# Token mixer with a second x buffer, first sums ahead of the second products, rows normalised by ScalarE, and weight preparation behind two maps

## Chip, cores and metric

The kernel runs on one core of a Trainium2 chip. The time is that of the whole program on the device, in microseconds, so lower is better. Engines are named as in the profile: PE is TensorE (matrix products), PEld its weight loads, DVE is VectorE, ACT is ScalarE, POOL is GpSimd, SP issues the loads and stores. The engines run their own instruction lists in order and meet only at semaphores.

## What is computed

The program runs a token mixer, a linear attention, a quantised feed-forward, an agent attention and a mixture of experts, one after the other. The change touches the token mixer and the first step of the attention. The mixer in the reference, shortened (8 batches of 256 rows, 4 heads of 64):

```python
q = proj(Wq_w, Wq_b)
k = proj(Wk_w, Wk_b)
v = proj(Wv_w, Wv_b)
ew = jnp.exp(w_bias * local_mask)
ek = jnp.exp(k)
num = jnp.einsum('ts,nsd->ntd', ew, ek * v)
den = jnp.einsum('ts,nsd->ntd', ew, ek)
y = jax.nn.sigmoid(q) * num / den
h = y @ out_w + out_b + _flatten(x)
mu = jnp.mean(h, axis=-1, keepdims=True)
var = jnp.mean(jnp.square(h - mu), axis=-1, keepdims=True)
return (h - mu) * jax.lax.rsqrt(var + 1e-05) * ln_g + ln_b
```

The attention maps q and k by elu(u) + 1, keeps a decayed running sum of k for its denominators, and multiplies its result by a gate. The feed-forward has a weight that is rounded to three values with a scale per row; its preparation (absolute sums, limits, comparisons, diagonals) is done once.

## The kernel before

**Order.** Each engine's list is written by hand. In `token_mixer` all engines go through the 8 batches by `skewed` (L70): it calls a function `step(b, s1, s2, s3)` for b = -2, -1, 0, then in a hardware loop for 1 to 5, then for 6 and 7. In step b an engine does the first part of batch b+2 (s1), the second part of batch b+1 (s2) and the third part of batch b (s3). `skewed` also places single pieces between the steps.

**A batch.** SP loads x transposed into `a_xt`, a single buffer (`load_x`, L194). TensorE makes q, k and v of all heads (`qkv_products`, L234, product L243) into the PSUM banks 0 to 3. ScalarE takes exp(k) into `a_nk` (L316) and exp(-q) into `a_eq` (L320); VectorE multiplies exp(k) by v (`weigh`, L361). TensorE multiplies both by exp(w_bias) (`sums`, L266). VectorE forms the denominator (`den`, L368), its reciprocal (L370) and `y` (L372). TensorE turns y (`turn`, L254), ScalarE copies it to `a_yt` (`copy_yt`, L325), TensorE multiplies by out_w (`project`, L277). VectorE adds x and the bias, prepared by POOL in `a_xb`, into `a_hp` (L379), takes mean and variance (L383, L387) and `ve` (L389). POOL raises that to -1/2 (`root`, L433), VectorE normalises two tiles into `a_hn` (L395), POOL applies gain and bias (`gain`, L438 and L440) and splits an eighth of the attention's weights (`split`, L446), whose rounded half ScalarE has cast (L336).

**Step b of each list.** TensorE: products of b+2, turn of b, sums of b+1, project of b. ScalarE: copy of b, exponentials of b+2, cast. VectorE: `weigh(b+2)`, `den` and `y` of b+1, then `norm(b)` (L379 to L395). POOL: root of b, xb of b+1, gain of b, split. Between steps 5 and 6 VectorE takes the statistics of the attention's first rows (`rows_sums(0)`), between steps 6 and 7 those of the next (`rows_sums(1)`), and ScalarE normalises the first rows with their text tile (`rows_norm(0)`, L570). After its last step ScalarE does `rows_round(0)` (L598) and `rows_norm(1)`; VectorE does `rows_split(0)` (L605) inside `norm(7)`, before the wait for the last root, and ends with the last gain and bias (L409, L411).

**First attention step.** A barrier parts the mixer from `attention_and_ffn`. Its step b = -1 runs the projections of batch 0 on TensorE: pairs 0 and the values, pair 1, the text values (which wait for the first map), pairs 2 to 5, then the products of `ffn_weights`. ScalarE takes exp and relu of each pair (L1092, L1096). VectorE makes the map `phi` from both (L1253), and behind it a scan (L1259) or a product with the running sum (L1264). In VectorE's list `ffn_weights` (L1298) stands ahead of `phi(0, 0)`; it waits for the feed-forward's weights, which SP loads after the barrier.

## Time and profile before

| what | us |
|---|---|
| median of three runs | 705.87 |
| lowest and highest run | 705.17, 706.28 |
| profiled execution, its time | 705.16 |
| profiled execution, its span | 703.4 |
| PE busy | 576.3 (82%) |
| DVE busy | 443.1 (63%) |
| ACT busy | 258.9 (37%) |
| POOL busy | 211.1 (30%) |

The profile is of one execution. The busy shares are means over stages with different limits: the mixer is the first 115 of the 703 us, and what bounds it has to be read there. Times in the trace are counted from the start of the span. A row of the timeline gives start and duration, the engine and the line of the kernel, output and inputs, how many instructions were merged, and in brackets how long the engine stood idle before it and whose end released it. The clock of TensorE is given as a share of 2.4 GHz; it has two levels, so 0.84 means that part of the stretch ran at 1.2 GHz. For the first 30 us the profile has no clock record, and the rate is to be read from the products themselves.

### The profile page before, as it was taken

To read this page: it belongs to the slowest core of one execution; us is meant where nothing else is said; L and a number is where in the kernel's file an instruction comes from. 1 tells how busy PE (TensorE), PEld (TensorE's weight loads), DVE (VectorE), ACT (ScalarE), POOL (GpSimd) and SP (SyncE) were. 2 spreads that over 40 slices of the span, in tenths; PEclk is the share of its full clock that TensorE was granted. 3 is DMA by queue.
4 is the path that set the end of the run, shared out by engine and by line. 5 is a ranking of instruction groups with operands and counts; after the bars stand their busy time and mean duration, and the time that the engine had idled before them with its cause. 6 is when DMAs were issued, how large, how long until landed. Compare 5 with 4: busy or idle time off the path is not lost. (4 is left out here: it accounts for less than half of the span.)

```text
span 703.4 us, 10705 instructions
## 1 busy us (share of the span) xinstructions
PE 576.3 (82%) x3633; PEld 458.8 (65%) x3633; DVE 443.1 (63%) x1037; ACT 258.9 (37%) x541; POOL 211.1 (30%) x283
## 2 busy tenths in 40 slices
PE   4889957789998999899998955452899799999883
PEld 4566535647685868677767643221688699988782
DVE  1388886666877878778887753457768442322256
ACT  1511222326372727263645323310441045554410
POOL 2336554121111111001111000461201277777600
PEclk9999987789999999999999986556899899999997
DMA  6211112000000000000000060310300133333376
GB/s 203 81 45 45 44 46 69 22 1 1 1 1 1 2 1 1 1 1 1 1 1 1 1 225 0 79 34 10 104 23 1 31 95 104 103 107 106 90 225 194
DMA packets 27439, 36.97 MB, mean 53 GB/s; under 512 B 4541, under 2 KB 22782, under 8 KB 27390
## 3 DMA queue, kind: packets, MB, share of 16 engines
q1 hardware_dynamic: 23166, 24.78, 11.5%
q0 software_dynamic: 4224, 11.54, 5.4%
q8 instruction: 30, 0.49, 0.3%
q14 instruction: 19, 0.16, 0.1%
HBM read 25.95 MB, written 10.35 MB: 52 GB/s over the span
## 5 line engine op out<-in xcount | busy, mean ns | idle before, releaser
L611 PE MATMUL ps<-b_x_hi,wa_hi 128*128 128x288 f32 x192 | 59.6, 310 | 6.9 <-DVE w1raw L1253 3.0
L1450 POOL TENSOR_TENSOR c_rstd<-c_ve,mhalf 128x2 f32<-128x2 f32 (+1 forms) x16 | 11.9, 742 | 165.2 <-DVE c_ve L510 165.2
L2373 DVE TENSOR_TENSOR w1raw<-ps,w1raw 128x192 f32<-128x192 f32 x43 | 15.4, 358 | 68.6 <-ACT w1raw L2174 68.6
L612 PE MATMUL ps<-b_x_lo,wa_hi 128*128 128x288 f32 x192 | 58.1, 303 | 0.0
L613 PE MATMUL ps<-b_x_hi,wa_lo 128*128 128x288 f32 x192 | 57.9, 302 | 0.0
L2433 POOL DMA_INDIRECT kv<-x_rows,r_src_i x43 | 41.8, 972 | 28.4 <-DVE r_src_i L2295 11.1
L2060 PE MATMUL ps<-w,w1raw 96*128 x172 | 44.7, 382 | 1.2 <-ACT w1raw L2186 1.2
L1497 POOL TENSOR_TENSOR w1raw<-w1raw 128x288 f32<-128x288 f32 x16 | 15.4, 981 | 98.5 <-DVE w1raw L1253 98.5
L1126 ACT CAST b_y_hi<-b_yt 128x256 fp32r<-128x256 f32 x32 | 12.8, 399 | 86.5 <-DVE b_yt L1235 86.5
L611 PEld LDWEIGHTS ps<-b_x_hi,wa_hi 128*128 128x128 f32 x192 | 37.5, 195 | 10.0 <-DVE w1raw L1253 4.3
L1247 DVE TENSOR_TENSOR w1raw<-ps,decay 128x1024 f32<-128x1024 f32 x32 | 38.6, 1205 | 7.5 <-PE ps L934 7.5
L934 PE MATMUL ps<-w1raw 64*128 64x160 f32 (+2 forms) x384 | 41.5, 334 | 1.2 <-DVE w1raw L1284 1.2
L1253 DVE SCALAR_TENSOR_TENSOR w1raw<-b_ex,w1raw 128x576 f32<-128x576 f32 x32 | 25.3, 791 | 21.2 <-ACT w1raw L1096 21.2
L612 PEld LDWEIGHTS ps<-b_x_lo,wa_hi 128*128 128x128 f32 x192 | 37.5, 195 | 0.3
L934 PEld LDWEIGHTS ps<-w1raw 64*128 64x128 f32 (+1 forms) x384 | 27.1, 162 | 16.3 <-issue 9.5
L613 PEld LDWEIGHTS ps<-b_x_hi,wa_lo 128*128 128x128 f32 x192 | 37.6, 196 | 0.0
L266 PE MATMUL ps<-a_nk,a_ewt 128*128 (+1 forms) x64 | 37.0, 732 | 0.0
L243 PE MATMUL ps<-a_wqkv,a_xt 65*128 65x192 f32 x128 | 27.5, 378 | 8.9 <-DMA a_wqkv<-in_wqkv 5.7
L951 PE MATMUL ps<-w1raw,b_v 128*64 128x288 f32 (+1 forms) x256 | 32.8, 380 | 0.8 <-DVE w1raw L1247 0.8
L611 PE MATMUL ps<-w_hi,f_w 128*128 x86 | 32.7, 380 | 0.8 <-DVE f_w L2304 0.8
L243 PEld LDWEIGHTS ps<-a_wqkv,a_xt 65*128 65x128 f32 x128 | 25.9, 226 | 10.1 <-DMA a_xt<-in_x_t 9.4
L1092 ACT ACTIVATE b_ex<-ps 128x576 f32<-128x576 f32 x32 | 20.9, 652 | 30.4 <-PE ps L613 30.4
(380 smaller groups left out, 1604.7 us busy)
## 6 DMA issues: line engine op xcount, KB each, us to landing
d_x_hi<-y_rows SPq DMA_DIRECT2D x18, 256.0 KB, 3.9
w1raw<-in_W_t SPq DMA_DIRECT2D x8, 384.0 KB, 6.0
x_rows<-w1raw SPq DMA_DIRECT2D x6, 384.0 KB, 2.5
a_xt<-in_x_t SPq DMA_DIRECT2D x8, 256.0 KB, 3.3
a_xfl<-in_x_flat SPq DMA_DIRECT2D x8, 256.0 KB, 2.7
out<-hres SPq DMA_DIRECT2D x16, 128.0 KB, 3.6
w<-in_W_t SPq DMA_DIRECT2D x8, 192.0 KB, 3.8
w1raw<-in_Ws_t SPq DMA_DIRECT2D x1, 768.0 KB, 10.3
```

The source lines that it names most:

```text
L243: mm = nc.tensor.matmul(qkv[:, lt, h, 0:3 * F], xt[:, h, lt * P:(lt + 1) * P], wqkv[:, :], start=True, stop=True)
L266: mm = nc.tensor.matmul(ps[:, 4 + t, :], ewt[:, s, t * P:(t + 1) * P], nk[:, b % 2, s, :], start=s == 0, stop=s == 1)
L611: nc.tensor.matmul(out, x_hi, w_hi, start=start, stop=False)
L612: nc.tensor.matmul(out, x_hi, w_lo, start=False, stop=False)
L613: return nc.tensor.matmul(out, x_lo, w_hi, start=False, stop=stop)
L934: mm = nc.tensor.matmul(ps[keys, bank(j) + r, col:col + n], qk[rows, NP + j, s * P:s * P + m], qk[rows, j, T - n:T], start=True, stop=True)
L951: mm = nc.tensor.matmul(ps[DK * r:DK * r + DK, 6 + j % 2, T - n:T], v[:, s, h * DK:(h + 1) * DK] if s < 2 else v_text[keys, h * DK:(h + 1) ...
L1092: nc.scalar.activation(ex[:, i % 2], ps[:, group(i):group(i) + 2, 0:T], ACT.Exp)
L1247: nc.vector.tensor_tensor(a[:, j % 2], ps[:, bank(j):bank(j) + 2, 0:AW], g["decay"][:, 2 * j:2 * j + 2, :], ALU.mult).then_inc(masked, 1)
L1253: nc.vector.scalar_tensor_tensor(out=qk[:, qk_tiles(i), 0:T], in0=ex[:, i % 2], scalar=1.0, in1=qk[:, qk_tiles(i), 0:T], op0=ALU.min, op1= ...
L2060: mm = nc.tensor.matmul(ps[:, 6 + u, 0:D], e_ht[:, u, k, :], w2[:, k, bass.ds(e, 1), :].rearrange("p a f -> p (a f)"), start=k == 0, stop= ...
L2433: pool.indirect_dma_start(xg[j % NX], None, x_rows, bass.IndirectOffsetOnAxis(ap=src_i[:, j:j + 1], axis=0)).then_inc(gathered[j % NX], 16)
```

## The change

Four things. `a_xt0` is a buffer of its own for batch 0, so that the load of batch 1 is issued with the first loads, without a wait, and batches 2 and later wait as before for the products of the batch ahead. In step -1, TensorE does the sums of batch 0 before the products of batch 1, and VectorE the division of batch 0 before `weigh(1)`. The rows are normalised by two ScalarE activations, scale and shift per row, at the end of ScalarE's step; VectorE adds the negated mean, POOL the product of it with the root. In the first attention step `ffn_weights` stands behind `phi(0, 0)` and `phi(0, 1)` in VectorE's list. Besides, `setup` uses one semaphore less.

```diff
@@ -116,6 +116,7 @@
         lng = sb("a_lng", [P, D])
         lnb = sb("a_lnb", [P, D])
         xt = sb("a_xt", [F + 1, H0, L])
+        xt0 = sb("a_xt0", [F + 1, H0, L])
         xfl = sb("a_xfl", [P, 2, D])
         xb = sb("a_xb", [P, 2, D])
         nk = sb("a_nk", [P, 2, 2, 2 * D])
@@ -131,6 +132,8 @@
         ve = sb("a_ve", [P, 2, 1])
         tick = sb("a_tick", [P, 1])
         rstd = sb("a_rstd", [P, 2, 1])
+        nmu = sb("a_nmu", [P, 2, 1])
+        shift = sb("a_shift", [P, 2, 1])
         lgam = sb("a_lgam", [P, HA])
         age = sb("a_age", [P, T])
         agm = sb("a_agm", [P, T])
@@ -140,6 +143,7 @@
         ln_in = sem("a_ln_in")
         ew_in = sem("a_ew_in")
         x_in = sem("a_x_in")
+        x0_in = sem("a_x0_in")
         xf_in = sem("a_xf_in")
         attw_in = sem("a_attw_in")
         txt_in = g["rows"]["txt_in"]
@@ -196,7 +200,11 @@
                     xs = x_t[b]
                 else:
                     xs = x_t[bass.ds(b, 1)].rearrange("a c h l -> (a c) h l")
-                ge(sp, qkv_done, b)
+                if isinstance(b, int) and b == 0:
+                    sp.dma_start(xt0[0:F], xs).then_inc(x0_in, 16)
+                    return
+                if not isinstance(b, int) or b > 1:
+                    sp.wait_ge(qkv_done, b)
                 sp.dma_start(xt[0:F], xs).then_inc(x_in, 16)
 
             def load_flat(b):
@@ -208,13 +216,13 @@
             sp.dma_start(wqkv[:], ins["wqkv"]).then_inc(w_in, 16)
             sp.dma_start(ewt[:], ins["w_bias_t"].rearrange("(s p) t -> p s t", p=P)).then_inc(ew_in, 16)
             sp.dma_start(mask8[:], ins["mask_t"].rearrange("(s p) t -> p s t", p=P)).then_inc(ew_in, 16)
+            load_x(1)
             sp.dma_start(draw[:], row_broadcast(ins["decay_log"], HA)).then_inc(gam_in, 16)
             sp.dma_start(outb[:], row_broadcast(ins["out_b"], D)).then_inc(ln_in, 16)
             sp.dma_start(outw[:], ins["out_w"].rearrange("(c p) n -> p c n", p=P)).then_inc(ln_in, 16)
             sp.dma_start(lng[:], row_broadcast(ins["ln_g"], D)).then_inc(ln_in, 16)
             sp.dma_start(lnb[:], row_broadcast(ins["ln_b"], D)).then_inc(ln_in, 16)
             load_flat(0)
-            load_x(1)
             for i, n in enumerate(("W_Q_t", "W_K_t", "W_V_t", "W_g_t")):
                 sp.dma_start(stage[:, :, i * DA:(i + 1) * DA],
                              ins[n].rearrange("(c p) n -> p c n", p=P)).then_inc(attw_in, 16)
@@ -232,22 +240,26 @@
         @block.tensor
         def _(pe):
             def qkv_products(b):
-                ge(pe, x_in, 16 * b + 16)
+                x = xt0 if isinstance(b, int) and b == 0 else xt
                 if isinstance(b, int) and b == 0:
+                    pe.wait_ge(x0_in, 16)
                     pe.wait_ge(filled, 1)
+                else:
+                    pe.wait_ge(x_in, 16 * b)
+                if isinstance(b, int) and b == 0:
                     pe.wait_ge(w_in, 16)
                 ge(pe, ekv_done, b)
                 ge(pe, exps_done, b)
                 for lt in range(2):
                     for h in range(H0):
-                        mm = nc.tensor.matmul(qkv[:, lt, h, 0:3 * F], xt[:, h, lt * P:(lt + 1) * P],
+                        mm = nc.tensor.matmul(qkv[:, lt, h, 0:3 * F], x[:, h, lt * P:(lt + 1) * P],
                                               wqkv[:, :], start=True, stop=True)
                 mm.then_inc(qkv_done, 1)
 
             def turn(b):
                 pe.wait_ge(y_done, b + 1)
                 if isinstance(b, int) and b == 0:
-                    pe.wait_ge(g["ident_ready"], 1)
+                    pe.wait_ge(g["ident_ready"], 2)
                 ge(pe, yt_done, b)
                 for fc in range(FC):
                     for t in range(2):
@@ -279,6 +291,10 @@
                 mm.then_inc(out_done, 1)
 
             def step(b, s1, s2, s3):
+                if isinstance(b, int) and b == -1:
+                    sums(0)
+                    qkv_products(1)
+                    return
                 if s1:
                     qkv_products(b + 2)
                 if s3:
@@ -319,6 +335,14 @@
                 ge(act, y_done, b - 1)
                 nc.scalar.activation(heads(eq[:, b % 2]), part(0), ACT.Exp, scale=-1.0).then_inc(exps_done, 1)
 
+            def norm(b):
+                act.wait_ge(rstd_done, 2 * b + 2)
+                ge(act, gain_steps, 2 * b)
+                for t in range(2):
+                    last = nc.scalar.activation(hn[:, t, :], hp[:, t, :], ACT.Identity, bias=shift[:, t, :],
+                                                scale=rstd[:, t, :])
+                last.then_inc(hn_done, 1)
+
             def copy_yt(b):
                 act.wait_ge(turned, b + 1)
                 ge(act, out_done, b)
@@ -334,6 +358,7 @@
                     if isinstance(b, int) and b == 0:
                         act.wait_ge(attw_in, 16 * 4)
                     nc.scalar.copy(part_of(g["wa_hi"], b), part_of(stage, b)).then_inc(hi_done, 1)
+                    norm(b)
 
             skewed(act, step, (rates, decays, None, lambda: rows_norm(nc, g, act, 0)))
             rows_round(nc, g, act, 0)
@@ -341,6 +366,7 @@
 
         @block.vector
         def _(dve):
+            nc.vector.memset(xt0[F:F + 1], 1.0)
             nc.vector.memset(xt[F:F + 1], 1.0).then_inc(filled, 1)
 
             def rates():
@@ -376,6 +402,7 @@
                 dve.wait_ge(out_done, b + 1)
                 dve.wait_ge(xb_done, b + 1)
                 ge(dve, hn_done, b)
+                ge(dve, rstd_done, 2 * b)
                 nc.vector.tensor_tensor(hp[:].rearrange("p t f -> p (t f)"), ps[:, 7, :],
                                         xb[:].rearrange("p t f -> p (t f)"), ALU.add).then_inc(hp_done, 1)
                 dve.wait_ge(hp_done, b + 1)
@@ -386,17 +413,16 @@
                 for t in range(2):
                     last = nc.vector.bn_aggr(mv[:, t, :], stats[:, t, :])
                 step(last)
+                nc.vector.tensor_scalar(nmu[:], mv[:, :, 0:1], -1.0, None, ALU.mult)
                 nc.vector.tensor_scalar(ve[:], mv[:, :, 1:2], LN_EPS, None, ALU.add).then_inc(var_done, 1)
                 if isinstance(b, int) and b == B - 1:
                     rows_split(nc, g, dve, 0)
-                dve.wait_ge(rstd_done, b + 1)
-                ge(dve, gain_steps, 2 * b)
-                for t in range(2):
-                    last = nc.vector.tensor_scalar(hn[:, t, :], hp[:, t, :], mv[:, t, 0:1], rstd[:, t, :],
-                                                   ALU.subtract, ALU.mult)
-                last.then_inc(hn_done, 1)
 
             def step(b, s1, s2, s3):
+                if isinstance(b, int) and b == -1:
+                    divide(0)
+                    weigh(1)
+                    return
                 if s1:
                     weigh(b + 2)
                 if s2:
@@ -432,6 +458,8 @@
                 pool.wait_ge(var_done, b + 1)
                 nc.gpsimd.tensor_tensor(rstd[:], ve[:], g["mhalf"][:, 0:2].rearrange("p (t a) -> p t a", a=1),
                                         ALU.pow).then_inc(rstd_done, 1)
+                pool.wait_ge(rstd_done, 2 * b + 1)
+                nc.gpsimd.tensor_tensor(shift[:], nmu[:], rstd[:], ALU.mult).then_inc(rstd_done, 1)
 
             def gain(b):
                 pool.wait_ge(hn_done, b + 1)
@@ -482,14 +510,13 @@
 def setup(nc, g):
 
     with ExitStack() as ctx:
-        zeroed = ctx.enter_context(nc.semaphore("zeroed"))
         block = ctx.enter_context(nc.Block())
 
         @block.gpsimd
         def _(pool):
             nc.gpsimd.memset(g["mhalf"][:], -0.5)
-            nc.gpsimd.memset(g["ident"][:], 0.0).then_inc(zeroed, 1)
-            pool.wait_ge(zeroed, 1)
+            nc.gpsimd.memset(g["ident"][:], 0.0).then_inc(g["ident_ready"], 1)
+            pool.wait_ge(g["ident_ready"], 1)
             nc.gpsimd.affine_select(out=g["ident"][:], in_=g["ident"][:], compare_op=ALU.not_equal,
                                     fill=1.0, base=0, pattern=[[-1, P]],
                                     channel_multiplier=1).then_inc(g["ident_ready"], 1)
@@ -1415,14 +1442,14 @@
                     rows_split(nc, g, dve, b + 2)
                 if is_batch(u):
                     scale(u)
-                if b == -1:
-                    ffn_weights()
                 if is_batch(n):
                     phi(n, 0)
                 if is_batch(b):
                     split_y(b)
                 if is_batch(n):
                     phi(n, 1)
+                if b == -1:
+                    ffn_weights()
                 if is_batch(u):
                     quantise(u)
                 if is_batch(n):
```

## Rows read from the trace of the kernel before

**Rows 1.** windows: length, busy PE, PEld, DVE, ACT, POOL (count), PEclk, DMA share, GB/s

```profile
50.51:61.36 10.85, 10.11 (x37) 6.67 (x37) 8.76 (x14) 2.08 (x4) 5.72 (x5) 0.84 0.20 49
61.36:71.03 9.67, 8.42 (x37) 6.01 (x37) 8.67 (x14) 2.08 (x4) 5.71 (x5) 1.00 0.20 54
```

**Rows 2.** timeline, short loop step: start, us, engine, line, operation [idle <-releaser]

```profile
60.61 0.69 DVE L372 TENSOR_TENSOR a_y<-ps,a_rden 128x512 f32<-128x512 f32 x1
...
61.85 3.60 PE L266 MATMUL ps<-a_nk,a_ewt 128*128 x8
...
62.05 0.59 ACT L325 COPY a_yt<-ps 128x512 f32<-128x512 f32 x1 [8.65 <-PE ps L254]
...
63.01 0.17 DVE L389 TENSOR_SCALAR a_ve<-a_mv 128x2 f32<-128x2 f32 x1
...
63.02 0.60 ACT L320 ACTIVATE a_eq<-ps 128x512 f32 x1
...
63.26 0.70 POOL L433 TENSOR_TENSOR a_rstd<-a_ve,mhalf 128x2 f32<-128x2 f32 x1 [4.39 <-DVE a_ve L389]
...
63.99 1.67 DVE L395 TENSOR_SCALAR a_hn<-a_hp,a_mv,a_rstd 128x256 f32<-128x256 f32 x2 [0.81 <-POOL a_rstd L433]
...
65.29 1.89 PE L277 MATMUL ps<-a_outw,a_yt 128*128 128x256 f32 x8
...
65.59 0.67 DVE L361 TENSOR_TENSOR a_nk<-a_nk,ps 128x512 f32 x1
...
66.19 0.68 DVE L368 SCALAR_TENSOR_TENSOR a_den<-a_eq,ps 128x512 f32<-128x512 f32 x1
```

**Rows 3.** timeline, VectorE in the step at 0.84 clock

```profile
56.50 0.69 DVE L368 SCALAR_TENSOR_TENSOR a_den<-a_eq,ps 128x512 f32<-128x512 f32 x1 [1.08 <-PE ps L266]
```

**Rows 4.** timeline, shift and normalising of attention rows on POOL and ScalarE

```profile
109.97 0.20 POOL L560 TENSOR_TENSOR b_shift<-b_nmu,b_rstd 128x2 f32<-128x2 f32 x1
...
110.25 1.09 ACT L570 ACTIVATE b_xn<-hres,b_shift,b_rstd 128x256 f32<-128x256 f32 x2
```

**Rows 5.** timeline, TensorE in the mixer's first 31 us

```profile
14.38 5.49 PE L243 MATMUL ps<-a_wqkv,a_xt 65*128 65x192 f32 x16 [3.19 <-DMA a_xt<-in_x_t]
...
19.66 5.56 PE L266 MATMUL ps<-a_nk,a_ewt 128*128 128x512 f32 x8
...
25.06 2.77 PE L243 MATMUL ps<-a_wqkv,a_xt 65*128 65x192 f32 x16
...
30.11 0.86 PE L254 MATMUL ps<-ident,a_y 128*128 128x128 f32 x4 [2.29 <-DVE a_y L372]
```

**Rows 6.** timeline, VectorE and ScalarE at the mixer's end

```profile
97.38 0.69 DVE L368 SCALAR_TENSOR_TENSOR a_den<-a_eq,ps 128x512 f32<-128x512 f32 x1
...
103.38 0.59 ACT L325 COPY a_yt<-ps 128x512 f32<-128x512 f32 x1 [0.78 <-PE ps L254]
...
107.88 0.68 DVE L379 TENSOR_TENSOR a_hp<-ps,a_xb 128x512 f32<-128x512 f32 x1
...
114.23 0.69 DVE L411 TENSOR_TENSOR hres<-a_hn,a_lnb 128x512 f32<-128x512 f32 x1
```

**Rows 7.** timeline, all engines in the first step of attention

```profile
119.40 0.66 ACT L1096 ACTIVATE w1raw<-ps 128x576 f32<-128x576 f32 x1
...
123.12 0.17 DVE L1304 COPY fold<-ident 32x32 f32<-32x32 f32 x1 [4.76 <-issue]
...
124.29 0.64 ACT L1096 ACTIVATE w1raw<-ps 128x576 f32<-128x576 f32 x1
...
127.43 0.75 DVE L1253 SCALAR_TENSOR_TENSOR w1raw<-b_ex,w1raw 128x576 f32<-128x576 f32 x1
...
131.84 0.61 PE L611 MATMUL ps<-b_x_hi,wa_hi 128*128 128x288 f32 x1 [0.68 <-ACT b_v_text L1116]
...
139.41 3.74 DVE L1264 TENSOR_TENSOR w1raw<-w1raw 128x288 f32<-128x288 f32 x2
...
143.30 0.69 PE L900 MATMUL ps<-w1raw,b_pick 128*32 128x288 f32 x8 [1.27 <-DVE w1raw L1264]
```

## Prediction

> **What bounds the kernel now.** The profile was read in this order: the page, for the share of each engine; the timeline of the token mixer, one loop step at a time, asking at each wait which of the awaited things came last; the granted clock of each loop step; the two ends of the mixer; the first step of the attention stage. All times are microseconds from the span's start.
>
> A mixer loop step runs from one `turn` to the next. Steps alternate between 9.67 and 10.85 us; in the long one the granted clock is 0.84, in the short one 1.00 [rows 1] (two of five such steps are shown). The five, from 40.79 to 91.55, take 50.76. In the short one VectorE is the bound: after `y` (60.61) come the sum with xb and the statistics up to `ve` (63.01), the wait for POOL's root (63.26), the two normalising instructions (63.99, 1.67 us), `weigh` (65.59), `den` (66.19) [rows 2]. TensorE had passed the sums that `den` needs at 65.29, when the first `project` product starts. In the long step the clock is low at the start of the sums and `den` begins 5.99 us after the turn at 50.51 [rows 3, 1]; VectorE has slack there. From `den` to the next `y` it is always 60.61 - 56.50 = 4.11 [rows 2, 3]. The reader is to see two nearly equal chains, TensorE's (turn, sums, den, y) and VectorE's own list, and ScalarE idle 8.65 us before its copy [rows 2]. That last number invites moving work there; what matters is where in ScalarE's order it goes.
>
> **Part 1, rows normalised by ScalarE.** Removed from VectorE: 1.67 us per batch and the wait of 0.81 for the root. Added: a small `nmu` operation (0.08, as those of two columns overlap), a `shift` on POOL, two ScalarE activations. The same pair exists for the attention rows: `shift` 0.20, ScalarE begins 0.28 after it, 1.09 for two tiles, the next instruction starting about 1.0 after the first [rows 4]. The catch is the order. ScalarE's step b ends with `norm(b)`; `norm(b)` needs `ve(b)`, and VectorE makes that after `y(b+1)`. Queued behind it are `copy_yt(b+1)` and `exps(b+3)`; VectorE's next instruction is `weigh(b+3)`, and `den(b+2)` stands behind that. So a ring closes through all four engines. One turn of it, from the start of `y`:
> to `ve` 2.40 (63.01 - 60.61), with `nmu` 2.48; to the root 0.25; root 0.70 and a gap near 0.08, so `shift` at 3.51; to ScalarE 0.25, so the rows at 3.76; two tiles 1.0, copy at 4.77; to the second exponential 0.97 (63.02 - 62.05), at 5.74; its 0.60 and 0.06 of hand-over, `weigh` at 6.40; `den` 0.60 later (66.19 - 65.59), at 7.00; 4.11 to the next `y`: **11.1 us** [rows 2 to 4].
> That is 0.95 more than the mean step of 10.15, whatever the clock does as long as the sums end before 7.0. Now the copy runs 1.44 after `y`; it will run at 4.8. The first such step moves `den(2)` from 45.7 to about 40.0 + 7.0 = 47.0; five more put `den(7)` at 102.5, against 97.38 [rows 6]: **+5.1**. Where the sums run wholly at the low clock they take twice the 3.4 from 61.85 to 65.29 [rows 2], 6.8, and `den` comes at about 8.1, 1.1 late; TensorE will idle 2.6 us a step (11.1 less 8.42 of work [rows 1]), so this can happen; bounds 0 to 5.5, taken 0.5, since the half-cold steps of before end at 6.7.
>
> The Trainium skill (TensorE: Matmul & The Clock Gate, the section on the array's architectural detail) says ScalarE, VectorE and GpSimdE are strictly first in, first out, which speaks against putting a late-fed instruction ahead of an early-fed one. If an engine could pass its waiting head, the step would be the 9.2 of the second rival below and not 11.1. [...]
>
> **Part 2, the mixer's end.** With D the start of `den(7)`: now the last copy starts at D+6.0, the last `hp` at D+10.5, the final sum at D+16.85 and ends at D+17.5 [rows 6]. After: `y(7)` D+4.1, `ve(6)` D+6.6, rows of batch 6 D+7.9, then the three tiles of `rows_norm(0)` (about 1.55 at the pair's rate), copy D+10.4, project at the low clock as now, `hp` D+14.9, `shift` D+17.9, rows of batch 7 D+18.2 to D+19.2. Behind them on ScalarE is `rows_round(0)`, behind that on VectorE `rows_split(0)` (832 columns each, against the 512 of the exponential's 0.60 and of `den`'s 0.68: estimates of 0.9 and 1.1), and then the final product and sum, 0.7 each: end D+22.4. **+4.9**. Of this, 4.4 is the copy behind `norm(6)` and the attention rows; the rest is the new place of `rows_round(0)`. Bounds +3.5 (project at the full clock) to +5.5.
>
> **Part 3, the start.** Batch 1's x no longer waits 3.19 us for the first products [rows 5], and the first sums come straight after `weigh(0)`, near 13.1 (products end 11.19; two exponentials and a product are 1.9 by rows 2). They take 5.2 to 6.8, `qkv(1)` 2.8 at the full clock (2.77) or 5.5 at the low one (5.49) [rows 5]. But `qkv(2)` needs batch 2's x, whose load waits for `qkv(1)` in the one remaining buffer and takes 3.2: 24.5 if the clock rises within the sums. The idle of 3.2 makes it fall, so `qkv(2)` takes 5.5 and the first turn, queued behind it, starts at about 30.0; it is 30.11 now [rows 5]. **0**, bounds -2.7 (qkv(2) at the full clock) and +1.5. The early `y(0)` is worth nothing. The extra memset of `xt0`, the 0.5 us that the small loads shift in SP's queue, and the weights of the attention (now not behind a waiting load) all lie under the first product and the first sums, and each would cost its own length without them.
>
> **Part 4, weight preparation behind two maps.** VectorE starts `ffn_weights` at 123.12, when its loads land, and ends at 127.43; only then comes `phi(0,0)`, whose input was ready at 120.06. TensorE waits for it, then for the copy of v_text behind it, and goes on at 131.84. `den` of the attention starts at 143.30 after the last z product (139.41 + 3.74) [rows 7]. After: `phi(0,0)` 120.1 to 122.2; `phi(0,1)` at 124.98 (its ScalarE input ends 124.93) to 127.1; `ffn_weights` 4.3 to 131.4; `phi(0,2)` and `phi(0,3)` 0.8 each to 133.0; z products 3.7 to 136.8; denominators at 136.9: -6.4. TensorE goes on near 125.7 (v_text copied behind the exponentials that end at 124.93) and has four pairs and the preparation's own products ahead of the denominators. These take 143.30 - 131.84 = 11.46 now, the wait at their end included, so 137.2 is a bound at today's pace; with all of it at the low clock, an estimate of 2 more, 139.2 (-4.1). Taken **-6.2**. What hides the moved block is the wait for pairs 2 and 3; of its 4.3 about 1 stays in front of `phi(0,2)`.
>
> **Sum.** 5.1 + 0.5 + 4.9 + 0 - 6.2 = +4.3. The profiled execution took 705.16 (span 703.4, 1.8 around it) and would take 709.5; the median of the runs is 705.87, 0.7 above, so 710.2.
>
> **Rivals.** First, the low clock wins: sums at half rate in most steps (+5 in all) or the pairs of the attention at half rate (-4.1): 712.5 to 716, centre 714. For it: more idle than any step of now; against it: half of the short-idle steps kept the clock. Chance 0.12.
> Second, on the other side: ScalarE's rows do not hold up its copy. Then VectorE is freed, the ring is TensorE's (turn 0.75 after `y`, first `project` product 3.93 later, 0.37 to `den`, 4.11 to `y`: 9.2), six steps give -6, the tail 0, part 4 -6.2: 693.5. It decides at `shift` being ready before the copy's input, that is `shift` under 1.4 after `y`; rows 2 and 4 put it at 3.5. Chance 0.07.
> Third, `qkv(2)` meets the full clock and 2.7 come off the start: 707.5. Chance 0.09.
> Fourth, the moved block does not do what it says: `phi(0,2)` behind it becomes the wait, half of part 4 is lost: 713. Chance 0.06. Fifth, small errors of one sign in ring and tail (0.3 a step, 1.5 in the tail) leave both parts even: 705 to 706.5, or just below. Chance 0.08.
> The rest, 0.58, is the forecast, with an own range of 707.5 to 712.5. Two in ten left out give 705.5 to 714. A change under 0.2% (1.4 us) can't be told from none here; faster 0.11, same 0.10, slower 0.79.
>
> **What would show it.** Loop steps of 11.1 with ScalarE's copy starting about 4.8 after `y`, released by nothing on TensorE; VectorE idle before `weigh`, on ScalarE; turn 0 near 30; the stage's end 10 later than 115; TensorE's wait for `phi(0,0)` gone and 22 us, not 28, from the stage's start to the denominators. Steps near 9.2 would refute the ring; a copy still 1.4 after `y` would show that the order was misread.

## The result

The changed kernel takes 717.1 us (median of four runs, 715.76 to 718.22) against 706.1 for the kernel before beside it: a ratio of 1.0136, with a 95% interval of 1.01 to 1.0172. The forecast had the sign and missed the size: +4.3 was forecast, +11 measured, and 717.1 lies above the range. The profiled executions have spans of 703.4 and 714.4; every trace named below is one execution.

| from the traces, us | before | after | difference |
|---|---|---|---|
| first turn | 30.11 | 30.50 | +0.4 |
| mixer loop steps (turn to turn), mean of the last six | 10.24 | 11.35 | |
| mixer's start to `den(7)` | 97.38 | 104.76 | +7.4 |
| `den(7)` to the attention's first product | 17.84 | 22.84 | +5.0 |
| from there to the first denominators | 28.07 | 21.34 | -6.7 |
| seven steps from these to the last denominators | 246.57 | 250.94 | +4.4 |
| from there to the end of the span | 313.5 | 314.5 | +0.95 |

Busy time tells little of this: VectorE has 11 us less and ScalarE 8 us more, and TensorE 7 us more for the same instructions. The first lines of the page after:

```profile
span 714.4 us, 10734 instructions
PE 583.3 (82%) x3633; PEld 461.5 (65%) x3633; DVE 431.7 (60%) x1030; ACT 266.9 (37%) x557; POOL 212.8 (30%) x291
```

One loop step after, in the timeline of all engines (start, duration, engine, line; `a_nk` of ScalarE is the first exponential, `a_eq` the second, VectorE's `a_nk` is `weigh`). It answers to [rows 2]:

```profile
52.20 0.69 DVE L398 TENSOR_TENSOR a_y<-ps,a_rden 128x512 f32<-128x512 f32 x1
...
54.67 0.16 DVE L417 TENSOR_SCALAR a_ve<-a_mv 128x2 f32<-128x2 f32 x1
...
54.92 0.71 POOL L459 TENSOR_TENSOR a_rstd<-a_ve,mhalf 128x2 f32<-128x2 f32 x1 [5.36 <-DVE a_ve L417]
...
55.70 0.20 POOL L462 TENSOR_TENSOR a_shift<-a_nmu,a_rstd 128x2 f32<-128x2 f32 x1
...
55.94 1.09 ACT L342 ACTIVATE a_hn<-a_hp,a_shift,a_rstd 128x256 f32<-128x256 f32 x2 [8.35 <-POOL a_shift L462]
...
56.93 0.56 ACT L349 COPY a_yt<-ps 128x512 f32<-128x512 f32 x1
...
57.55 1.99 PE L289 MATMUL ps<-a_outw,a_yt 128*128 128x256 f32 x8 [0.51 <-ACT a_yt L349]
...
57.89 0.59 ACT L336 ACTIVATE a_eq<-ps 128x512 f32 x1
...
58.87 0.69 DVE L387 TENSOR_TENSOR a_nk<-a_nk,ps 128x512 f32 x1 [4.03 <-ACT a_eq L336]
...
59.47 0.68 DVE L394 SCALAR_TENSOR_TENSOR a_den<-a_eq,ps 128x512 f32<-128x512 f32 x1
```

The reader is to see the ring in it. From `y` at 52.20 every row but TensorE's `project` is released by the one above it or stands behind it in its engine's list, across VectorE, POOL, ScalarE and VectorE again, and the next `y` is at 63.57. ScalarE is idle 8.35 us before its rows, and the copy, whose input was there at about 53.6, starts at 56.93, behind them. TensorE's `project` waits for that copy. The idle VectorE (4.03 us before `weigh`) is the price.

The mixer's end, ScalarE and VectorE, which answers to [rows 6]:

```profile
104.76 0.69 DVE L394 SCALAR_TENSOR_TENSOR a_den<-a_eq,ps 128x512 f32<-128x512 f32 x1 [2.09 <-PE ps L278]
...
112.58 1.09 ACT L342 ACTIVATE a_hn<-a_hp,a_shift,a_rstd 128x256 f32<-128x256 f32 x2 [9.13 <-POOL a_shift L462]
...
113.58 1.08 ACT L597 ACTIVATE b_xn<-hres,b_shift,b_rstd 128x256 f32<-128x256 f32 x2
...
115.06 0.56 ACT L349 COPY a_yt<-ps 128x512 f32<-128x512 f32 x1
...
119.49 0.69 DVE L406 TENSOR_TENSOR a_hp<-ps,a_xb 128x512 f32<-128x512 f32 x1 [5.70 <-PE ps L289]
...
123.61 0.83 ACT L625 CAST b_x_hi<-ps 128x832 fp32r<-128x832 f32 x1
...
124.47 1.02 DVE L632 TENSOR_TENSOR b_x_lo<-ps,b_x_hi 128x832 fp32r<-128x832 f32 x1 [2.94 <-ACT b_x_hi L625]
...
126.12 0.69 DVE L437 TENSOR_TENSOR hres<-a_hn,a_lnb 128x512 f32<-128x512 f32 x1
```

The last copy (115.06) stands behind the rows of batch 6 (112.58) and the attention's first rows (113.58); `rows_round(0)` (123.61) and `rows_split(0)` (124.47) stand ahead of the final two products. From `den(7)` the copy is at 10.3, `hp` at 14.7, the end at 22.0: the forecast had 10.4, 14.9 and 22.4.

The attention's first step, VectorE, with one row of ScalarE and two of TensorE, answering to [rows 7]:

```profile
132.46 0.76 DVE L1280 SCALAR_TENSOR_TENSOR w1raw<-b_ex,w1raw 128x576 f32<-128x576 f32 x1 [1.73 <-ACT w1raw L1123]
...
138.31 0.76 DVE L1280 SCALAR_TENSOR_TENSOR w1raw<-b_ex,w1raw 128x576 f32<-128x576 f32 x1 [3.65 <-ACT w1raw L1123]
...
141.55 0.65 ACT L1123 ACTIVATE w1raw<-ps 128x576 f32<-128x576 f32 x1
...
144.74 1.54 DVE L1280 SCALAR_TENSOR_TENSOR w1raw<-b_ex,w1raw 128x576 f32<-128x576 f32 x2
...
145.54 0.41 PE L638 MATMUL ps<-b_x_hi,wa_hi 128*128 128x288 f32 x1 [1.41 <-DVE w1raw L1280]
...
148.94 0.69 PE L927 MATMUL ps<-w1raw,b_pick 128*32 128x288 f32 x8
```

The first map runs 4.9 after the stage's start, the second at 10.7, the third and fourth behind the weight preparation at 17.1; the denominators are 21.3 after the start, forecast 21.7. The moved block (140.44 to 144.74) does hold something up: the third map's input is ready at 142.20 (141.55 + 0.65), the map starts behind the block at 144.74, and TensorE waits 1.41 us for it, until 145.54. Up to the denominators the kernel was 5.6 us behind the one before. The rest was lost later, where the change touches nothing.

### The profile page after: what moved, and what is told of

Its sections match the earlier page's. It is cut to its first block and busy times, and to the rows that moved or that the text cites. A ratio compares the mean times of both kernels' runs of the same rounds, so it can differ in the third digit from the quotient of the medians.

```text
span 714.4 us, 10734 instructions
## 1 busy us (share of the span) xinstructions
PE 583.3 (82%) x3633; PEld 461.5 (65%) x3633; DVE 431.7 (60%) x1030; ACT 266.9 (37%) x557; POOL 212.8 (30%) x291
## 5 line engine op out<-in xcount | busy, mean ns | idle before, releaser
L2460 POOL DMA_INDIRECT kv<-x_rows,r_src_i x43 | 41.8, 972 | 28.4 <-DVE r_src_i L2322 11.1
L961 PE MATMUL ps<-w1raw 64*128 64x160 f32 (+2 forms) x384 | 44.6, 352 | 1.2 <-DVE w1raw L1311 1.2
L1524 POOL TENSOR_TENSOR w1raw<-w1raw 128x288 f32<-128x288 f32 x16 | 16.1, 1027 | 94.5 <-DVE w1raw L1280 94.5
L961 PEld LDWEIGHTS ps<-w1raw 64*128 64x128 f32 (+1 forms) x384 | 29.0, 173 | 17.6 <-issue 10.5
L1280 DVE SCALAR_TENSOR_TENSOR w1raw<-b_ex,w1raw 128x576 f32<-128x576 f32 x32 | 25.3, 790 | 20.6 <-ACT w1raw L1123 20.5
L342 ACT ACTIVATE a_hn<-a_hp,a_shift,a_rstd 128x256 f32<-128x256 f32 x16 | 8.7, 593 | 68.0 <-POOL a_shift L462 68.0
```

The source lines that it names most:

```text
L961: mm = nc.tensor.matmul(ps[keys, bank(j) + r, col:col + n], qk[rows, NP + j, s * P:s * P + m], qk[rows, j, T - n:T], start=True, stop=True)
L1280: nc.vector.scalar_tensor_tensor(out=qk[:, qk_tiles(i), 0:T], in0=ex[:, i % 2], scalar=1.0, in1=qk[:, qk_tiles(i), 0:T], op0=ALU.min, op1= ...
L2460: pool.indirect_dma_start(xg[j % NX], None, x_rows, bass.IndirectOffsetOnAxis(ap=src_i[:, j:j + 1], axis=0)).then_inc(gathered[j % NX], 16)
```

## Experiments

Each run's difference is to the changed kernel unless it says otherwise. Ratios are to the kernel before, run on the same chip. The runs were made on more than one chip; on that of `e5_late_rows`, `e6_copy_first`, `e7_prep_alone` and `e8_delay` the last stage takes some 23 us more (its expert products stand idle 15.8 us in `e5_late_rows` against 1.2 in the changed kernel's trace; the reason was not looked for), so times of these are compared by ratio, and stages ahead of that by their traces.

### The ring

`e2_vector_rows`: rows back on VectorE, the rest of the change kept. The negated mean, the shift and the wait for it go as well; those lines are not printed here.

```diff
-                    norm(b)
...
+                dve.wait_ge(rstd_done, b + 1)
+                ge(dve, gain_steps, 2 * b)
+                for t in range(2):
+                    last = nc.vector.tensor_scalar(hn[:, t, :], hp[:, t, :], mv[:, t, 0:1], rstd[:, t, :],
+                                                   ALU.subtract, ALU.mult)
+                last.then_inc(hn_done, 1)
```

> The changed kernel with only the rows given back to VectorE (its two normalising instructions, no negated mean, no shift). Ring theory (the wait for the rows ahead of ScalarE's copy makes the 11.36 us step and the longer end): steps return to 9.7 and 10.9, the stage ends near 115.5 in place of 127.6, and with the moved preparation worth 6.7 the time is 705.9 - 6.7 = about 699, 18 below the changed kernel if the later loss goes with it, 12 below if it stays. Rival (the steps are long because TensorE's clock falls in its longer idle): steps stay above 10.9 and the time stays above 710.

Measured: 701.5 us, ratio 0.9941 (0.9898 to 0.9984); the traced execution took 697.7, near the lowest of ten runs that reach 706.2. The loop's steps are 9.66 to 9.72, the mixer's end is at 114.4, 13.2 earlier than in the changed kernel. The rival falls, and by the changed kernel's own steps: one at the full clock takes 11.37, and the two behind 64.32 and 75.67, which begin with TensorE partly at 1.2 GHz, take 11.35 and 11.36.

```profile
52.95:64.32 11.37, 8.93 (x37) 5.84 (x37) 7.16 (x13) 3.05 (x6) 5.88 (x6) 1.00 0.15 49
64.32:70.00 5.68, 5.68 (x13) 2.64 (x14) 1.77 (x8) 2.71 (x6) 3.37 (x4) 0.70 0.12 39
75.67:81.00 5.33, 5.33 (x12) 2.86 (x13) 1.78 (x8) 2.35 (x5) 3.28 (x4) 0.68 0.17 49
```

`e11_rows_in_four`: the dose.

```diff
-                for t in range(2):
-                    last = nc.scalar.activation(hn[:, t, :], hp[:, t, :], ACT.Identity, bias=shift[:, t, :],
+                for t, c in ((0, 0), (0, 1), (1, 0), (1, 1)):
+                    c = slice(c * P, (c + 1) * P)
+                    last = nc.scalar.activation(hn[:, t, c], hp[:, t, c], ACT.Identity, bias=shift[:, t, :],
```

> The changed kernel with the rows of a batch normalised by four ScalarE activations of 128 columns in place of two of 256: the same result, about 0.5 us more on ScalarE per batch. Ring theory: every loop step grows by that, 11.36 to about 11.9, and the mixer ends 3 to 4 later. Rival (TensorE's clock sets the step): steps unchanged, since ScalarE idles 8 us in each.

Measured: 716.9 us, ratio 1.015 (1.0114 to 1.0187). ScalarE in one step of it:

```profile
68.99 1.65 ACT L343 ACTIVATE a_hn<-a_hp,a_shift,a_rstd 128x128 f32<-128x128 f32 x4 [8.30 <-POOL a_shift L463]
...
70.55 0.56 ACT L350 COPY a_yt<-ps 128x512 f32<-128x512 f32 x1
```

The copy starts 1.56 after the rows, not 0.99, so 0.57 of dose; the steps went from 11.36 to 11.90, by 0.54. The ring takes the dose one for one, with ScalarE idle 8.3 us in the step. The mixer ended 4.9 later, more than the 3 to 4 expected (its second turn was already 0.6 later), yet the whole was no slower; that is taken up below.

`e5_late_rows`: the ring cut by order. Step 1 is written out besides, on all engines; those lines are not printed here.

```diff
                 if s3:
+                    if not isinstance(b, int) or b > 0:
+                        norm(b - 1)
...
                     nc.scalar.copy(part_of(g["wa_hi"], b), part_of(stage, b)).then_inc(hi_done, 1)
-                    norm(b)
+                    if isinstance(b, int) and b == B - 1:
+                        norm(b)
```

> The changed kernel with ScalarE's rows of batch b moved one place on in its list: behind the copy of batch b+1 and the exponentials of batch b+3, so that nothing that feeds VectorE or TensorE stands behind their wait (step 1 is written out on all engines, so that the loop runs from 2). Ring theory: the ring is cut, VectorE is freed of 2.5 us a step, and the step is TensorE's 9.2 (0.75 from y to the turn, 4.3 to den, 4.1 to y); six steps save 2.2 each against the changed kernel, the copy of batch 7 no longer waits (4.4), about 17.5 in all: stage end near 110, time about 700 with the attention's later batches as they are, 696 if they find a better place against the clock. Rival (ScalarE's rows cost by themselves, in whatever place): steps stay near 11.

Measured: 720.1 us against 730.5 for the kernel before on that chip, ratio 0.9867 (0.9817 to 0.9917). The same instructions as in the changed kernel, in another place of ScalarE's list, in one step:

```profile
58.71 0.69 DVE L402 TENSOR_TENSOR a_y<-ps,a_rden 128x512 f32<-128x512 f32 x1
...
60.14 0.59 ACT L350 COPY a_yt<-ps 128x512 f32<-128x512 f32 x1 [5.26 <-PE ps L267]
...
61.11 0.60 ACT L337 ACTIVATE a_eq<-ps 128x512 f32 x1
...
62.11 0.69 DVE L391 TENSOR_TENSOR a_nk<-a_nk,ps 128x512 f32 x1 [0.73 <-ACT a_eq L337]
...
62.47 1.09 ACT L343 ACTIVATE a_hn<-a_hp,a_shift,a_rstd 128x256 f32<-128x256 f32 x2 [0.75 <-POOL a_shift L466]
...
63.76 0.69 DVE L398 SCALAR_TENSOR_TENSOR a_den<-a_eq,ps 128x512 f32<-128x512 f32 x1 [0.95 <-PE ps L279]
```

The copy is 1.43 after `y`, the rows behind the exponentials, `den` waits for TensorE's sums, and the loop's steps are 9.16, the value worked out for TensorE's ring. The mixer ended at 112.3, 15.3 earlier than in the changed kernel, not 17.5: the last step took 11.7, since TensorE meets its last sums at the low clock, and the last `project` was no faster.

`e12_late_rows_again` is the same kernel on another chip, for the experiments further down.

> The kernel of e5_late_rows itself, beside the one with the delay and on the same chip. Loop steps of 9.16, mixer's end near 112.3; seven steps near 252 if the place against the clock repeats, as it did in the three traces with the long ring; ratio to the kernel before near 0.987.

Measured: 697.6 us, ratio 0.9883 (0.9852 to 0.9915), steps 9.16. The mixer ended at 114.0, not near 112.3, its second turn being 1.5 later already. The seven later steps took 247.6, where `e5_late_rows` had 252.1: the place did not repeat, against what was expected.

### The end and the start of the mixer

`e6_copy_first`: the attention's first rows behind the last copy.

```diff
                     copy_yt(b)
+                if isinstance(b, int) and b == B - 1:
+                    rows_norm(nc, g, act, 0)
...
-            skewed(act, step, (rates, decays, None, lambda: rows_norm(nc, g, act, 0)))
+            skewed(act, step, (rates, decays, None, None))
```

> The changed kernel with only the attention's first rows (three tiles on ScalarE) moved behind the last copy. The last copy starts 6.2 us after the last y, of which these tiles are 1.5. If the path runs through that copy: the mixer ends 1.5 earlier (126.1 in place of 127.6), steps of 11.36 stay. Rival (the end is set by the product behind it at the low clock, or by the clock's next change): less than 0.8 earlier. The time of the whole is less sure, since the later batches meet the clock elsewhere: 713 to 717.

Measured: from the last turn to the attention's first product 16.5 us against 18.0, so the 1.5 of the three tiles; the mixer ended at 125.3. The steps stayed at 11.36. The ratio is 1.0114 (1.006 to 1.0169), no clear gain, for the seven later steps took 252.1 in this trace.

`e4_old_start`: the start as before. In SP's part, not printed here, the load of batch 1 waits again and stands behind the small loads.

```diff
-                if isinstance(b, int) and b == -1:
-                    sums(0)
-                    qkv_products(1)
-                    return
...
-                if isinstance(b, int) and b == -1:
-                    divide(0)
-                    weigh(1)
-                    return
```

> The changed kernel with the start as before: batch 1's load waits for the first products and stands behind the small loads, products of batch 1 ahead of the first sums, division of batch 0 behind weigh of batch 1. The first turn was at 30.11 before and at 30.50 in the changed kernel, the second at 40.79 and 41.51. If the new start is worth nothing: within 1 us of the changed kernel, perhaps 0.5 faster. If the early first sums had hidden something: 2 to 3 us slower.

Measured: 715.2 us, ratio 1.0127 (1.0038 to 1.0216); first turn 30.28, second 40.94, against 30.50 and 41.51, and 31.21 and 42.37 in `e1_after_again`. The new start is worth nothing and may cost a little: over the ten traces that have it the second turn is at 40.8 to 42.8 (mean 41.9), over the four with the old start at 40.8 to 42.0 (mean 41.3). The start of TensorE in the changed kernel shows why, answering to [rows 5]:

```profile
13.26 5.84 PE L278 MATMUL ps<-a_nk,a_ewt 128*128 128x512 f32 x8 [1.94 <-DVE a_nk L387]
...
18.93 2.77 PE L255 MATMUL ps<-a_wqkv,a_xt 65*128 65x192 f32 x16
...
25.22 5.49 PE L255 MATMUL ps<-a_wqkv,a_xt 65*128 65x192 f32 x16 [3.53 <-DMA a_xt<-in_x_t]
...
30.50 1.06 PE L266 MATMUL ps<-ident,a_y 128*128 128x128 f32 x4
```

The sums come 6.4 us earlier than before and the products of batch 1 run in 2.77, at the full clock. Then TensorE waits 3.53 for batch 2's x, the clock is down again (5.49 for the same products), and the turn, whose input was ready at 24.0, stands behind them.

### The moved preparation

`e3_prep_ahead` puts it back in the changed kernel; `e7_prep_alone` moves it in the kernel before. The edit of the second:

```diff
-                if b == -1:
-                    ffn_weights()
                 if is_batch(n):
                     phi(n, 0)
...
                     phi(n, 1)
+                if b == -1:
+                    ffn_weights()
```

> The changed kernel with only the weight preparation put back ahead of both maps. If the move is worth what the first trace shows (21.3 against 28.1 us from the stage's start to the denominators): 6 to 7 us slower than the changed kernel, about 723.5. If the later low-clock stretches follow from it (TensorE's phase against the clock): only 1 to 2 us slower, and no low stretches in excess behind 160 us.

> The kernel before with only the weight preparation moved behind the two maps. From the stage's start to the denominators 21.3 in place of 28.1; time 705.9 - 6.7 = about 699. If the gain is lost again behind the denominators (low clock in the later batches): 702 to 706. It also tells what the rest of the change costs by itself: changed kernel less this one, about 18.

Measured: `e3_prep_ahead` 720.5 us, ratio 1.0202 (1.0113 to 1.0292), 27.0 from the stage's start to the denominators against 21.2 in `e1_after_again` beside it; 2.9 us slower than that, neither the 6 to 7 nor the 1 to 2 expected: 5.8 were lost ahead of the denominators, and 2.7 came back, since its seven later steps took 248.2 and not 250.9. `e7_prep_alone` has a ratio of 0.9885 (0.9844 to 0.9926), 20.2 us to the denominators, and later steps of 246.55, as before. The move is a gain by itself: 5.8 to 7.9 us ahead of the denominators in three pairs of traces, and 5 to 11 by the interval of `e7_prep_alone`.

### Where the rest went

`e1_after_again`: the changed kernel, no edit.

> The changed kernel itself, unaltered, for a second trace. In its first trace the attention's denominators start 5.6 us later than before, but the span ends 11.0 later; the other 5.4 come in the attention's later batches, in three stretches of low granted clock more than before (3.4 at 188, 6.8 at 222, 3.4 at 335). Theory A (those stretches fall by where the work happens to lie against the clock's changes): the mixer's steps and its end repeat within 0.2 us, the low stretches behind 160 us lie elsewhere, and the time still comes out at 715 to 718, because some are met in any run. Theory B (the change shifts every later batch into them): the stretches come at the same places again.

Measured: 717.6 us, ratio 1.0153 (1.0063 to 1.0242). The batches of the attention's denominators in windows, from one L927 (L900 before) to the next, for three steps and for all seven. First the kernel before:

```profile
core 0: us, PE busy (x) PEld busy (x) DVE busy (x) ACT busy (x) POOL busy (x), PEclk, DMA share, GB/s
143.30:177.32 34.02, 30.53 (x223) 22.69 (x223) 22.15 (x38) 13.76 (x26) 3.40 (x17) 0.90 0.01 1
177.32:211.44 34.12, 31.80 (x259) 25.32 (x258) 26.18 (x52) 17.01 (x32) 3.89 (x6) 1.00 0.00 1
211.44:246.61 35.17, 32.14 (x261) 25.55 (x261) 27.57 (x60) 17.26 (x32) 4.93 (x8) 1.00 0.01 1
143.30:389.86 246.56, 226.09 (x1796) 179.48 (x1796) 189.19 (x402) 119.13 (x217) 30.35 (x61) 0.98 0.00 1
```

The changed kernel, with one stretch inside the third step:

```profile
148.94:182.77 33.83, 30.34 (x223) 22.82 (x222) 22.09 (x38) 14.99 (x28) 6.41 (x19) 0.90 0.00 1
182.77:218.40 35.63, 33.31 (x260) 26.31 (x259) 26.21 (x52) 17.02 (x32) 3.88 (x6) 0.95 0.00 1
218.40:256.62 38.22, 35.19 (x262) 27.74 (x261) 27.63 (x60) 17.26 (x32) 4.93 (x8) 0.91 0.00 1
222.40:229.20 6.80, 6.80 (x32) 5.23 (x34) 3.23 (x7) 0.00 (x0) 0.00 (x0) 0.50 0.00 0
148.94:399.88 250.94, 230.47 (x1798) 182.56 (x1797) 189.21 (x402) 120.37 (x219) 33.35 (x63) 0.96 0.00 1
```

Its second trace, the third step, the stretch in it and all seven:

```profile
219.49:257.70 38.21, 35.18 (x261) 27.79 (x260) 27.64 (x60) 17.24 (x32) 4.92 (x8) 0.91 0.01 1
223.40:230.20 6.80, 6.80 (x32) 5.27 (x34) 3.17 (x7) 0.00 (x0) 0.00 (x0) 0.50 0.00 0
150.11:400.99 250.88, 230.41 (x1798) 182.68 (x1797) 189.23 (x402) 120.35 (x219) 33.31 (x63) 0.96 0.00 1
```

VectorE's busy time in the third step is the same in all (27.6); TensorE's instructions are the same, but in the changed kernel it spends 6.8 us of the step at 0.50, that is 1.2 GHz, and the step takes 38.2 in place of 35.2. The stretches at 0.50 repeat in the second trace, and not at the same time but at the same work: 60.7 and 94.8 us after the attention's first product in one, 60.4 and 94.5 in the other, 60.5 and 94.6 in `e4_old_start`. So neither A nor B held as written: the mixer's steps repeated but for one of 12.0, its end came 1.3 later and not within 0.2, and the low stretches moved with the work. The place repeats in runs without a trace too: the eight runs of the changed kernel, in two sets, have spans of 714.0 to 716.5 and mean granted clocks of 0.890 to 0.892, where twelve of the thirteen of the kernel before beside the second set spread over 698.6 to 708.6, with 0.894 to 0.916.

Is that a cost of the batches themselves? `e8_delay` has one useless instruction more:

```diff
             dve.wait_ge(hn_done, B)
+            nc.vector.reciprocal(rden[:, 0:1, :], den[:, 0:1, :])
             nc.vector.tensor_tensor(hn[:], hn[:], twice(lng), ALU.mult).then_inc(gain_steps, 1)
```

> The changed kernel with a useless reciprocal of 256 columns (about 1.7 us) on VectorE ahead of the mixer's last two products; nothing else. It moves the attention stage later by about 1.3 (127.6 to 128.9) and changes no work in it. In three traces the seven steps between the attention's denominators took 250.9 in all, against 246.6 in the kernel before. Theory A (those 4.3 come from where the batches lie against the clock's changes, and the mixer's end sets that place): with the shift the seven steps take another time, 246 to 249, and the whole is no slower than the changed kernel, perhaps 2 us faster, though it does more. Theory B (the 4.3 are a cost of the change itself, wherever the batches lie): 250.9 again and 1.3 us slower.

```profile
150.14:183.73 33.59, 30.09 (x224) 22.76 (x223) 22.11 (x38) 14.99 (x28) 6.43 (x19) 0.90 0.01 1
183.73:219.43 35.70, 33.38 (x260) 26.53 (x259) 26.16 (x52) 16.99 (x32) 3.87 (x6) 0.95 0.00 1
219.43:254.59 35.16, 32.14 (x261) 25.56 (x260) 27.55 (x60) 17.23 (x32) 4.91 (x8) 1.00 0.00 1
150.14:397.84 247.70, 227.24 (x1798) 180.77 (x1797) 189.15 (x402) 120.27 (x219) 33.30 (x63) 0.97 0.00 1
```

The low stretch of the second step lies 59.6 us behind the attention's first product, where the three traces without the delay have 60.4 to 60.7, and that of the third step is gone: it has the full clock and 35.16 us. The seven take 247.7, 3.2 less; the agent attention's last products (the "agent stage" below) start at 486.2, 2.5 earlier than in the changed kernel, although the mixer ends 1.7 later. So what theory A said came, and the 250.9 of B did not; the same work has no such cost in another place. `e11_rows_in_four` has it too, unasked: 4.9 later at the mixer's end, its seven steps took 247.7, and the whole is no slower than the changed kernel. That the delay makes the whole faster is not shown: its ratio is 1.0071 (1.0034 to 1.0107), those without it are 1.0136 and 1.0153, the intervals overlap, and no run of the changed kernel stands beside it on its chip.

Two more with the delay, one on the late rows, one on the kernel before. The edit of the first against `e5_late_rows`; the second has that of `e8_delay`:

```diff
+            nc.vector.reciprocal(rden[:, 0, 0:192], den[:, 0, 0:192])
```

> The kernel of e5_late_rows with a useless reciprocal of 192 columns (about 1.25 us) on VectorE ahead of the mixer's last two products. In e5 the mixer ended at 112.3, but the seven steps between the attention's denominators took 252.1, against 246.6 in the kernel before, and the way from the last denominators to the agent stage 90.1 against 88.3. Placement theory (what the later batches take is set by where they lie against the clock's changes): the stage starts 0.8 to 1 later, the seven steps take 246.5 to 248, and the whole is 4 to 6 us faster than e5 in spite of the added work. Cost theory (late rows make the later batches slower): 252 again and 0.8 us slower than e5.

> The kernel before with the useless reciprocal of 256 columns (1.7 us) ahead of the mixer's last two products, and nothing of the change. Placement theory: the kernel before is in a good place (246.6 for the seven steps) and loses it: they take 248 to 251, the whole is 3 to 6 us slower, two to three times the added work. Otherwise: 246.6 again and 1.7 us slower.

Measured: `e9_late_rows_delay` 696.9 us, ratio 0.9861 (0.983 to 0.9892), seven steps 246.5 and 88.3 to the agent stage. Against `e12_late_rows_again` beside it (247.6, 697.6) that is 1 us in the traces and nothing sure in the times; the 252.1 of `e5_late_rows` did not come again, so the 4 to 6 us were not there to be won, and the pair says nothing on the delay. `e10_before_delay`: 707.8 us, ratio 1.0033 (0.9994 to 1.0073), seven steps 246.7. The kernel before did not fall into a bad place; the expectation of 248 to 251 was wrong. From the last turn to the attention's first product it is 1.6 longer, the delay's own length; in the whole the interval leaves anything from nothing to 5 us.

| trace | seven steps | of these TensorE at 1.2 GHz | to the agent stage |
|---|---|---|---|
| before, `e10_before_delay`, `e7_prep_alone`, `e2_vector_rows`, `e9_late_rows_delay` | 246.5 to 246.7 | 10.2 | 88.2 to 88.4 |
| `e8_delay`, `e11_rows_in_four`, `e12_late_rows_again`, `e3_prep_ahead` | 247.6 to 248.2 | 13.7 | 88.3 to 89.1 |
| after, `e1_after_again`, `e4_old_start` | 250.9 | 20.5 | 88.8 |
| `e5_late_rows`, `e6_copy_first` | 252.1 | 23.9 | 90.1 to 90.2 |

The same work thus takes 246.5 to 252.1 us, and the order of the rows is that of the time at the low clock, summed from the clock records of each trace: about 0.4 us for each us of it (5.5 over 13.7, an estimate from the first and last rows). `e5_late_rows` and `e12_late_rows_again` are one kernel in two rows, so the code alone does not set the row. The three traces of kernels with both the mixer's end and the first attention step of the change sit in the third row; one with a delay, a dose or the preparation put back does not. That the mixer's end brings the work to the same place each time (the clock is low there in all three, for 10.2 us from the last turn on, and rises while TensorE is the bound, which would pull early and late runs together) is argued from these rows, not tested by itself.

## Why the prediction was wrong

**The ring: right, 1.5 too small.** The step that builds it gave 11.1 and the loop made 11.36. Up to the second exponential the rows agree to 0.1 (5.69 after `y`, forecast 5.74). The mis-sized term is the hand-over from ScalarE to `weigh`: forecast 0.06, measured 0.39 (57.89 + 0.59 to 58.87). No row stands behind the 0.06; outside the loop, where this hand-over is the last wait as well, it takes 0.04 (before, from 31.98 + 0.60 to 32.62). Six times 0.27 is 1.6. The 0.5 for sums at the low clock was right in kind: `e1_after_again` has one step of 12.0, 0.64 over, with the clock low for 6.8 us. With the start's 0.4 to 0.7 later and that 0.5 not met in this trace, `den(7)` moved by 7.4 in place of 5.6.

**The end: right.** +5.0 against +4.9, each piece within 0.4; `e6_copy_first` took out the 1.5 of the attention's rows as worked out.

**The start: right.** 0 forecast, 0 to +1 measured, by the mechanism given; 24.5 was said for batch 2's x and it was 25.2.

**The preparation: right in size, not all of it in mechanism.** -6.7 against -6.2; the denominators at 21.3 after the stage's start against 21.7. The forecast had about 1 us of the moved block in front of `phi(0,2)`, hidden; it was 2.5 (142.20 to 144.74), and TensorE waited 1.41 for it. That is the fourth rival's wait, at less than half of its price of 3. And the forecast put VectorE's products and TensorE within 0.3 of each other at the end; in the trace VectorE has ended at 148.23 and the denominators start at 148.94, straight behind TensorE's other products.

**The sum: the step that failed.** It ended at the first denominators and put everything behind them at nothing, without a reason. There 5.3 us were lost (4.4 in the seven steps, 0.6 up to the agent stage, 0.35 behind), since TensorE spent 20.5 us of the seven unchanged steps at 1.2 GHz and not 10.2. The miss of 6.7 is these 5.3, 1.8 up to `den(7)` and 0.1 in the end, less 0.5 in the preparation. The range's upper end, 714, was built from a low clock inside the mixer and the first step of the attention; that the same low clock could cost in the seven unchanged steps stood nowhere, though [rows 1] had shown steps of one loop differing by 1.2 us for no other reason. The windows of the kernel before, had they been taken there, show it too: 0.90 in its first step behind the denominators, 1.00 in the next two. The 5.3 are of one pair of traces; the medians differ by the same 11.0 as the spans.

**The rivals.** The one on the other side (693.5 if the rows do not hold up the copy) was a true picture of a kernel with another order: `e5_late_rows` has its 9.16. Its condition here was `shift` under 1.4 after `y`, and 3.50 was measured. The first rival's range, 712.5 to 716, comes nearest to the 717.1, but not by its mechanism: the low clock cost its 5 us behind the mixer, in steps that it did not name.

**The order rule.** A copy with its input ready waited 3.3 us behind rows that were not (53.6 to 56.93), and the dose of `e11_rows_in_four` went through one for one. The trace agrees with what the Trainium skill says of ScalarE's queue, that it is strictly first in, first out (TensorE: Matmul & The Clock Gate, the section on the array's architectural detail). Of the clock the rows show less: the steps of the changed kernel from 64.32 and 75.67 were entered after 1.8 and 1.2 us of idle, and their first 5.7 and 5.3 us have a granted clock of 0.70 and 0.68; the step from 52.95 was entered after 1.8 us as well and has 1.00.

A version that beats both kernels came out of it: the change with ScalarE's rows behind the exponentials of the next step, 0.9867, 0.9883 and, with the delay, 0.9861 of the kernel before. The preparation alone gives 0.9885, so the rest of the change, even cut free of the ring, adds nothing that these runs can tell: its mixer ended at 112.3 and 114.0, against 115.2 and 116.9 in the two traces with that of the kernel before, and the seven steps behind took 252.1 and 247.6 against 246.6.

## What to carry over

When work is moved to an idle engine, write out that engine's list and ask for each of its instructions when the input comes: one that is fed late and stands ahead of one that is fed early ties the engines into a ring, and the ring's length, not the busy time, is the new loop step. Moving it behind the early ones gave 2.2 us a step here. A sum that stops at the last changed stage needs a term for the stages behind it where TensorE's clock changes: here up to 5.6 us for the same instructions, of either sign.

## What the runs showed that was not expected

The same attention steps, the same instructions, take 246.5 to 252.1 us depending on how long TensorE's clock is low in them (10.2 to 23.9 us), and the one trace with an instruction of 1.7 us that does nothing reached the agent stage 2.5 us earlier than the trace without it. The last wait before VectorE's `weigh` in the hardware loop costs 0.39 us from ScalarE's end, where the same hand-over outside the loop takes 0.04 (in the changed kernel from 33.17 to 33.21). It goes with the loop and not with the batch: `weigh(3)` starts 0.42 behind ScalarE in the loop of the changed kernel (47.08 to 47.50), and 0.04 behind it in all three traces of the late rows, where step 1 is written out (43.57 to 43.61 in `e5_late_rows`). Why is not shown.
